# Expert products in one uniform loop over tiles of 128 rows, with the rows stationary in gate and up

## What the kernel must compute

```python
xs = jnp.repeat(x, K, axis=0)[sort_idx]                 # rows sorted by expert, K = 8
gate = jax.lax.ragged_dot(xs, w_gate, group_sizes)      # 1024 -> 512
up   = jax.lax.ragged_dot(xs, w_up, group_sizes)        # 1024 -> 512
down = jax.lax.ragged_dot(jax.nn.silu(gate) * up, w_down, group_sizes)   # 512 -> 1024
routed = (down[unsort].reshape(T, K, H) * tkw[..., None]).sum(axis=1)
shared = jax.nn.silu(x @ sw_gate) * (x @ sw_up) @ sw_down                # 1024 -> 1024 -> 1024
```

## Time and profile before

| | us |
|---|---|
| median of 3 runs | 13802.49 (13787.64 to 13813.24) |
| the profiled execution, its span | 13802.6 |
| TensorE matmul busy | 12644.3 (92%) |
| VectorE busy | 4582.2 (33%) |
| ScalarE busy | 2663.1 (19%) |
| GpSimd (POOL) busy | 2921.7 (21%) |
| mean granted clock of TensorE | 0.955 of full speed |

### The profile page before, as it was taken

How to read it: one execution, slowest core, us unless ns; L and a number is a source line. 1 busy time by engine, 2 the same in 40 slices (tenths; PEclk the granted TensorE clock), 3 DMA queues, 4 the chain that set the end, 5 groups by cost and what they waited for, 6 DMA issues and landing times. The chain is left out here.

```text
span 13802.6 us, 174940 instructions
## 1 busy us (share of the span) xinstructions
PE 12644.3 (92%) x58832; PEld 10259.1 (74%) x58833; DVE 4582.2 (33%) x7170; ACT 2663.1 (19%) x3851; POOL 2921.7 (21%) x2566
## 2 busy tenths in 40 slices
PE   4477699999999999999999998999998999999998
PEld 3333288888878888788878787878877777788787
DVE  8877722222222222222232223232323323222222
ACT  1133211111111211112121112121212212111111
POOL 3222233343321111111111111111111111111111
PEclk7678799999999999999999999999999999999999
DMA  5311222232232232333332323232333333322322
GB/s 188 123 55 70 88 58 60 64 75 61 61 79 61 70 75 61 75 76 88 68 90 61 74 64 101 60 90 60 95 74 100 104 73 89 75 60 61 75 60 48
DMA packets 286514, 1059.44 MB, mean 77 GB/s; under 512 B 52301, under 2 KB 52749, under 8 KB 262510
## 3 DMA queue, kind: packets, MB, share of 16 engines
q0 software_dynamic: 211040, 689.25, 23.7%
q1 hardware_dynamic: 75278, 367.17, 7.2%
HBM read 607.86 MB, written 448.40 MB: 77 GB/s over the span
## 5 line engine op out<-in xcount | busy, mean ns | idle before, releaser
L1236 POOL DMA_INDIRECT out_rows<-y,idx_cur x656 | 1034.4, 1577 | 7783.6 <-DVE y L1397 5070.1
L1442 PE MATMUL pg<-x_hi,w_hi 128*128 128x512 f32 (+2 forms) x5664 | 2161.0, 382 | 298.2 <-issue 212.6
L1471 PE MATMUL pd<-w_hi,a_hi 128*128 128x512 f32 x5248 | 2159.9, 412 | 0.0
L1443 PE MATMUL pg<-x_lo,w_hi 128*128 128x512 f32 (+2 forms) x5664 | 2154.4, 380 | 0.0
L1444 PE MATMUL pg<-x_hi,w_lo 128*128 128x512 f32 (+2 forms) x5664 | 2152.4, 380 | 0.0
L1442 PE MATMUL pu<-x_hi,w_hi 128*128 128x512 f32 (+2 forms) x5664 | 2131.7, 376 | 0.0
L1444 PE MATMUL pu<-x_hi,w_lo 128*128 128x512 f32 (+2 forms) x5664 | 2131.7, 376 | 0.0
L1443 PE MATMUL pu<-x_lo,w_hi 128*128 128x512 f32 (+2 forms) x5664 | 2131.7, 376 | 0.0
L1471 PE MATMUL pd<-w_hi,a_lo 128*128 128x512 f32 x5248 | 2062.9, 393 | 0.0
L1471 PE MATMUL pd<-w_lo,a_hi 128*128 128x512 f32 x5248 | 2048.3, 390 | 0.0
L1362 DVE TENSOR_TENSOR av<-pu,sg 128x512 f32<-128x512 f32 (+1 forms) x708 | 471.3, 666 | 4472.4 <-ACT sg L1296 4051.1
(11 more groups left out here) (240 smaller groups left out, 10975.1 us busy)
## 6 DMA issues: line engine op xcount, KB each, us to landing
stage<-in_w_all SPq DMA_DIRECT2D x186, 1024.0 KB, 4.8
xt<-in_x SPq DMA_DIRECT2D x16, 2048.0 KB, 12.9
xn_rows<-xn SPq DMA_DIRECT2D x16, 2048.0 KB, 6.7
base_rows<-bs SPq DMA_DIRECT2D x16, 2048.0 KB, 8.4
base<-base_rows SPq DMA_DIRECT2D x64, 512.0 KB, 5.6
out_rows<-base SPq DMA_DIRECT2D x64, 512.0 KB, 2.6
xraw<-xn_rows,idx_next POOLq DMA_INDIRECT x656, 5.4
out_rows<-y,idx_cur POOLq DMA_INDIRECT x656, 6.1
```

The source lines that it names most:

```text
L1236: g.indirect_dma_start(out=out, out_offset=bass.IndirectOffsetOnAxis(ap=idx_cur[:, j, 0:1], axis=0), in_=y[:, j % 2], in_offset=None, comp ...
L1442: m(dst, hi[:, cols], x[0][xs], start=first, stop=False)
L1443: m(dst, hi[:, cols], x[1][xs], start=False, stop=False)
L1471: last = m(pd[k % 2][:], wa[:, i, j * P:(j + 1) * P], wb[4 + h][:, i * 512:(i + 1) * 512], start=i == 0 and part == 0, stop=i == KI - 1 an ...
```

## The change

Work is one loop over tiles of 128 rows (`tile(t, q)`, two tiles a turn, 672 places of which those without work are passed over by a condition, `through`). In gate and up the tile's rows are the stationary operand and 512 columns of weights move, so the hidden values come out with the rows over partitions and the activations `av` are turned by four transposes on TensorE before they are split. TensorE's order in a tile is gate(t), half the transposes of rows t+1, up(t), the other half, down(t-1), activations of t. Weights are laid out anew: pieces 0 and 1 are gate, 2 and 3 up, 4 and 5 down. SP loads the table's entries two tiles ahead; POOL copies them, gathers rows two tiles ahead and adds the tile before; it scatters 16 times ahead of each pair of tiles until all 512 are issued. The split of the next expert's four pieces stands behind both copies of the next rows. `plan_stage` works on 128 partitions with five places each and passes its lists through DRAM. The short bodies, `by_tiles` and the lists of tile counts go.

Only added lines are shown; what they replace is in the listing above.

```diff
+def wait_past(eng, sem, value, passed=None):
+    if not isinstance(value, int) or value > 0:
+        if passed:
+            wait_apart(eng, passed, sem, value)
+        else:
+            eng.wait_ge(sem, value)
...
@@ plan_stage: five lists for 640 places, five to a partition
+        @block.sync
+        def _(sp):
...
+            sp.wait_ge(done, PLAN_STEPS)
+            for n in range(5):
+                sp.dma_start(plan_d[n].rearrange("(p f) -> p f", p=P), rows_i[n][:]).then_inc(listed, 16)
+            sp.wait_ge(listed, 16 * 5)
+            for n, row in enumerate(plan):
+                sp.dma_start(row[:, NSH:NSH + P * NF], plan_d[n:n + 1]).then_inc(listed, 16)
+            sp.wait_ge(listed, 16 * 10)
...
@@ expert_stage
+        def through(eng, passed, tile, rest=None):
+            def one(t, q):
+                with eng.If(value_of(eng, kinds, t, 2) > 1):
+                    tile(t, q)
+                with eng.Else():
+                    if rest:
+                        with eng.If(value_of(eng, kinds, t, 2) > 0):
+                            rest(t, q)
+                        with eng.Else():
+                            eng.sem_inc(passed, 1)
+                    eng.sem_inc(passed, 1)
+            for q in range(2):
+                tile(q, q)
+            with eng.Fori(1, NB // 2) as i:
+                for q in range(2):
+                    one(i * 2 + q, q)
...
+            def load(t, qs):
+                e = value_of(sp, experts, t, E + SH - 1)
+                run = value_of(sp, runs, t, E + SH, 1)
+                for q in qs:
+                    sp.wait_ge(split_lo, run * NCH + q)
+                    sp.dma_start(stage[q % NST][:], w_all[bass.ds(e * NCH + q, 1)]
+                                 .rearrange("a p c -> (a p) c")).then_inc(staged[q % NST], 16)
+            def slots_of(t, q):
+                first = value_of(sp, starts, t + 2, (E + SH) * T)
+                sp.wait_ge(idx_copied, t + 1)
+                sp.dma_start(idx_g[q][:], table[bass.ds(first, P)]).then_inc(idx_loaded[q], 16)
+            def tile(t, q):
+                slots_of(t, q)
+                with sp.If(value_of(sp, fresh, t + 1, 1) > 0):
+                    load(t + 1, (3, 4, 5))
+                with sp.Else():
+                    sp.sem_inc(sp_passed, 1)
+                with sp.If(value_of(sp, fresh, t + 2, 1) > 0):
+                    load(t + 2, (0, 1, 2))
+                with sp.Else():
+                    sp.sem_inc(sp_passed, 1)
+                sp.sem_inc(sp_passed, 1)
...
+            for q in range(2):
+                slots_of(q, q)
+            with sp.Fori(1, NSH // 2 - 1) as i:
+                for q in range(2):
+                    tile(i * 2 + q, q)
+            sp.wait_ge(scattered, NSC * SC * 16)
...
+            def scatter(n):
+                if not isinstance(n, int):
+                    wait_apart(pool, pool_passed, scattered, n * (SC * 16))
...
+                for j in range(SC):
+                    g.indirect_dma_start(
+                        out=table, out_offset=bass.IndirectOffsetOnAxis(ap=slot_cur[:, j:j + 1], axis=0),
+                        in_=payload_cur[:, j], in_offset=None).then_inc(scattered, 16)
+            def gather(t, q, half):
+                wait_apart(pool, pool_passed, idx_loaded[q], half * 16 + 32)
+                wait_apart(pool, pool_passed, tx_done, t * 2 + 2)
+                g.indirect_dma_start(out=xraw[q][:], out_offset=None, in_=xn_d,
+                                     in_offset=bass.IndirectOffsetOnAxis(ap=idx_g[q][:, 0:1], axis=0))\
+                    .then_inc(gathered[q], 16)
+            def add(t, q):
+                wait_apart(pool, pool_passed, y_ready, t * 2 + 2)
+                wait_past(pool, added, t * 16, pool_passed)
+                g.indirect_dma_start(out=out, out_offset=bass.IndirectOffsetOnAxis(ap=idx_s[q][:, 0:1], axis=0),
+                                     in_=y[q][:], in_offset=None, compute_op=ALU.add).then_inc(added, 16)
+            def copied(t, q, half):
+                wait_apart(pool, pool_passed, idx_loaded[q], half * 16 + 16)
+                wait_past(pool, added, (t - 1) * 16, pool_passed)
+                g.tensor_copy(idx_s[q][:], idx_g[q][:]).then_inc(idx_copied, 1)
+            def tile(t, q, half):
+                copied(t, q, half)
+                wait_apart(pool, pool_passed, idx_copied, t + 1)
+                gather(t, q, half)
+                if not (isinstance(t, int) and t == 0):
+                    add(t - 1, 1 - q)
+            for q in range(2):
+                tile(q, q, 0)
+            scatter(0)
+            with pool.Fori(1, NSC) as i:
+                scatter(i)
+                for q in range(2):
+                    tile(i * 2 + q, q, i)
+            with pool.Fori(NSC, NB // 2) as i:
+                for q in range(2):
+                    t = i * 2 + q
+                    with pool.If(value_of(pool, kinds, t, 2) > 1):
+                        tile(t, q, i)
+                    with pool.Else():
...
+            def tile(t, q):
+                if not (isinstance(t, int) and t == 0):
+                    a_high(t - 1)
+                act.wait_ge(gate_done, t + 1)
+                wait_past(act, av_ready, t)
+                a.activation(sg[:], pg[:], ACT.Silu).then_inc(sg_ready, 1)
+                x_high(t + 1, 1 - q, 0)
+                x_high(t + 1, 1 - q, 1)
+                with act.If(value_of(act, fresh, t, 1) > 0):
+                    run = value_of(act, runs, t, E + SH)
+                    wait_past(act, down_done, t * 2)
+                    for k in (4, 5):
+                        high(run, k)
+                with act.Else():
+                    act.sem_inc(act_passed, 1)
+                with act.If(value_of(act, fresh, t + 1, 1) > 0):
+                    run = value_of(act, runs, t + 1, E + SH)
+                    for k in range(4):
+                        if k == 2:
+                            act.wait_ge(up_done, t + 1)
+                        high(run, k)
+                with act.Else():
+                    act.sem_inc(act_passed, 1)
+                act.sem_inc(act_passed, 1)
+            for k in range(4):
+                high(0, k)
...
+            def tile(t, q):
+                begun = not (isinstance(t, int) and t == 0)
+                if begun:
+                    a_low(t - 1)
+                x_low(t + 1, 1 - q, 0)
+                dve.wait_ge(sg_ready, t + 1)
+                dve.wait_ge(up_done, t + 1)
+                wait_past(dve, ta_done, t)
+                v.tensor_tensor(av[:], pu[:], sg[:], ALU.mult).then_inc(av_ready, 1)
+                x_low(t + 1, 1 - q, 1)
+                with dve.If(value_of(dve, fresh, t, 1) > 0):
+                    run = value_of(dve, runs, t, E + SH)
+                    for k in (4, 5):
+                        low(run, k)
+                    wait_apart(dve, dve_passed, split_lo, run * NCH + (6 + NST - 1))
+                with dve.Else():
+                    dve.sem_inc(dve_passed, 1)
+                dve.sem_inc(down_weights, 1)
+                with dve.If(value_of(dve, fresh, t + 1, 1) > 0):
+                    run = value_of(dve, runs, t + 1, E + SH)
+                    for k in range(4):
+                        low(run, k)
+                    wait_apart(dve, dve_passed, split_lo, run * NCH + (4 + NST - 1))
+                with dve.Else():
+                    dve.sem_inc(dve_passed, 1)
+                dve.sem_inc(gu_weights, 1)
+                if begun:
+                    for h in range(2):
+                        scaled(t - 1, 1 - q, h)
...
+            def turn_rows(t, q, h, half):
+                if h == 0:
+                    pe.wait_ge(gathered[q], half * 16 + 16)
+                wait_past(pe, xl_ready, (t - 1) * 2 + h + 1)
+                for k in range(4):
+                    last = nc.tensor.transpose(tx[h][:, k], xraw[q][:, (4 * h + k) * P:(4 * h + k + 1) * P],
+                                               ident[:])
+                last.then_inc(tx_done, 1)
+            def product(dst, hi, lo, whi, wlo, cols, begin, end):
+                m(dst, hi, whi[:, cols], start=begin, stop=False)
+                m(dst, hi, wlo[:, cols], start=False, stop=False)
+                return m(dst, lo, whi[:, cols], start=False, stop=end)
...
+            def down(t):
+                pe.wait_ge(al_ready, t + 1)
+                pe.wait_ge(down_weights, t + 1)
+                wait_past(pe, y_ready, t * 2)
...
+            def tile(t, q):
+                pe.wait_ge(xl_ready, t * 2 + 2)
+                pe.wait_ge(gu_weights, t + 1)
+                wait_past(pe, sg_ready, t)
+                hidden(pg, q, 0).then_inc(gate_done, 1)
+                turn_rows(t + 1, 1 - q, 0, ahead_of(t, q))
+                wait_past(pe, av_ready, t)
+                hidden(pu, q, 2).then_inc(up_done, 1)
+                turn_rows(t + 1, 1 - q, 1, ahead_of(t, q))
```

(11 more changed lines are left out.)

## The result

The changed kernel takes 14435.1 us (median of 4; before 13804.5 in the same runs): ratio 1.0456, 95% interval 1.0441 to 1.0471, 4.6% slower. 14160 was forecast: direction and range hold, the loss is 631 us and not 356.

What follows compares the result with a forecast made beforehand. TensorE was taken to set the pace; first gate 1690, tiles 11677, scatter circle 365, expert changes 385 and end 42 sum to 14159 us. Forecast 14160 us, 2.6% slower, range 13,800 to 14,530.

Steps and rivals of the forecast that it cites:

- The steady tile: One tile on TensorE, 72 matmuls and 12 transposes: 17.8 us, or 11677 us for 656 tiles.
- the start: Plan and first rows before the first gate: first gate at 1690 us in place of 1720.
- the end: Stretch after the last matmul, with 15 skipped tiles: 42 us, where the old one took 30.6.
- the order of operands: TensorE's matmul spacing does not depend on which operand stands still: 0.227 us each, 16.34 us for 72.
- The circle: POOL's add, scatters, index copy and gather, then TensorE: 46.5 us per two tiles against 35.6, over tiles 2 to 63; 365 us.
- Change of expert: Gate waits for the new expert's weight splits at 30 changes, 11.5 us each, plus 5 × 8 for one-tile experts: 385 us.
- Rival A: Neither new wait shows, as POOL gets ahead or the splits hide: 13470 us, 2.4% faster; chance 0.10.
- B: Rival: one of the two new waits, scatters or expert change, hides: 13835 or 13795 us; chance 0.12.
- C: Rival: the circle of add, index and gather binds every tile, even without scatters: 14,870 us; chance 0.10.
- D: Rival: TensorE's closing branch fetches code at each loop end, 6.9 us for 328 closings: 16,400 us; chance 0.03.
- The intended gain: Padded columns and variant bodies of short blocks go from TensorE's stream: 11677 us against 12052, a gain of 375 us.

Runs made afterwards that it cites:

- the early signal: The changed kernel, but VectorE signals gate's and up's weights before splitting down's two pieces where no new expert follows; 14157.9 us.
- both repairs: The changed kernel with VectorE's signal ahead of down's split and four scatters behind each tile; 13866.5 us, ratio 1.0050.
- the last version: On both repairs: gate and up each wait for their own pieces, gate's next pieces are split in the old expert's last tile; 13572.5 us, ratio 0.9836.

## Why the forecast came out right, and short

- The steady tile, the start and the end were right within 31 us in all (10, 20 and 1), and so was the reading that the order of operands is free.
- The circle was right in place, number and size: 353 us up to tile 62 and some 15 in tile 63 for 365, gathers landing in 3.9 us as taken, and smaller groups take it away.
- The size that was off is the term "Change of expert", 385 us against 677. Its first pause is as worked out (10.2 us for 9.8). The step that failed is its last sentence, "Down's two pieces of the new expert are ready some 30 us after the new tile starts at worst, 6 us before its down runs". That is true (26.5 us in the timeline above), and it asks only who waits for those pieces. The next signal for gate stands behind their split on VectorE, and that was the later one: 25 more waits of 7.7 us with a slow restart, 229 us from tile 63 on by the early signal, and one more in tile 1. It was counted only for experts of one tile (5 × 8). With both repairs 465 us are left at the changes, 80 above 385. They are in one-tile experts, where two chains of splits follow each other (with the early signal these tiles are 40.3 to 41.6 us long, 22.5 to 23.8 above 17.77, for about 19.5 counted), in 12.6 us on the mean for an ordinary change in place of 11.5, and in waits of 0.4 to 2.4 us for `xraw` two or three tiles after a change.
- Rival A fell with the first timeline; B needed one wait hidden, and neither was. C: most tiles from 64 on are 17.77, so the circle without scatters hides. D: TensorE's closing branch takes 0.18 us at most, as this row of the source view of 5000 to 5600 us shows (min/median/max ns), and 0.21 us in the whole run, where the earlier trace rows left it open. Below it are two rows of the DMA queues (packets, MB, share). The first is a queue that moved instructions in the kernel before, from 1750 to 13772 us; the second is all that moved instructions in the changed kernel, from 1750 to 14393 us:

```profile
L1123 PEldq COMPARE_BRANCH  x63: 67/169/177, 5004.2 to 5599.6; - x63
...
q8 instruction: 164, 2.69, 0.1%
...
q14 instruction: 3, 0.02, 0.0%
```

So D's mechanism was real, but in the kernel before: 15 of its 191 closing branches took 4.1 to 6.9 us, and the queue moved a packet in each of the 15 and in none of the other 176, which took 0.24 us at most. In the changed kernel that queue is silent. (The forecast took the loop's body for two thirds of a full block's code; it has 168 matmuls and transposes against 320, about half.)

- The intended gain was real: in the last version the stage takes 11845 us (656 × 17.77 and 188 of excess), against 12052 before. Of the forecast's 375 us from short blocks 207 show, and only once POOL's group and VectorE's order are repaired.

## What to carry to other kernels

When work is recast as one uniform loop, every rare branch in it (a new expert, a batch of scatters) sits in an engine's queue ahead of the next signal: for each operation in such a branch ask not only who needs its result but which signal is issued behind it, and give that signal first, where it is already true. A batch that was hidden over four tiles isn't hidden over two; cut it to what one tile's slack holds. And let a consumer wait for the part that it reads first.

## What the runs showed that was not expected

Moving one signal on VectorE changed what TensorE does in tiles 3 to 63. With the early signal and scatters still in groups of 16, TensorE stops inside a gate, between matmuls that wait for no semaphore, and ScalarE and VectorE stand still with it until some 3 us after the last scatter, though the transposes that ScalarE's `a_hi` reads were done at 2023.9 us:

```profile
2026.61 0.40 PE L1380 MATMUL pg<-w_hi,x_lo 128*128 128x512 f32 x1 [0.85 <-issue]
...
2028.71 0.39 PE L1378 MATMUL pg<-w_hi,x_hi 128*128 128x512 f32 x1 [1.71 <-issue]
...
2030.33 0.20 POOL L1214 COPY idx_s<-idx_g 128x2 int32<-128x2 int32 x1
...
2031.53 0.59 PE L1379 MATMUL pg<-w_lo,x_hi 128*128 128x512 f32 x1 [2.42 <-issue]
...
2033.16 1.41 DVE L1313 TENSOR_SCALAR y<-pd,idx_s 128x512 f32<-128x512 f32 x2 [13.03 <-remote]
2033.24 0.60 ACT L1257 ACTIVATE a_hi<-ta 128x512 fp32r<-128x512 f32 x1 [13.83 <-remote]
```

The version with doubled transposes shows this in every pair too (194 us of "issue" beside its 7.9 us ahead of tile 1), that with four scatters a group hardly (6 us, before 1750 us), and the changed kernel, that with eight and those with both repairs not at all. It lies in time that TensorE would have spent waiting for the gather, so it cost nothing here, and pairs were even 1.6 us closer with it.

An obvious guess is that instructions come late while POOL's scatters are under way. The DMA queues speak against a fetch: from 1800 to 3110 us the version with the early signal moved no packet of an instruction queue, while TensorE waited 182 us for "issue". No run here tests anything else, nor why one small edit brings it on, and both stay open.
